# All experts but the last in fp16 halves, and a new split of the low halves between GpSimd and VectorE

## The chip, the cores and the metric

The kernel runs on one core of a Trainium2 chip. A core has TensorE (PE, matrix products into PSUM), VectorE (DVE), ScalarE (ACT), GpSimd (POOL, which reads and writes SBUF only) and SyncE (SP, which issues most of the DMAs here). Each engine works through its own queue in order and waits on semaphores for the others. The metric is the device time of one execution in microseconds (us); the median of 3 runs of the kernel before is 131.86 us (131.57 to 131.89).

## The reference

2048 tokens of 128 numbers (32 sequences of 64) pass through one attention layer and one mixture of experts:

```python
x = x + xattn(ctx, layernorm(x), Wq)          # q = xn Wq^T, k = v = ctx Wq^T, scores / sqrt(128), causal softmax in each sequence of 64
xf = layernorm(x)
logits = xf @ gate_W                          # 8 experts
gates = softmax(logits); top-2, renormalised  # cw[token, expert]
out = xf
for e in range(8):
    h = relu(xf @ W1[e] + b1[e])              # 128 -> 256
    out = out + cw[:, e:e+1] * (h @ W2[e] + b2[e])   # 256 -> 128
x = x + out
```

The kernel puts two sequences of 64 into a tile of 128 tokens, and a mask keeps them apart. It computes every expert for every token and weighs the result, so that the work does not depend on the routing.

## The kernel before, in words

The 2048 tokens are 16 tiles of 128, in four groups of four tiles (`GROUPS = 4`, 512 tokens each). Group 0's attention comes first, in a start part (roughly the first 20 us). Then a loop runs over the groups g and over the eight experts e; between the experts of group g it carries out, in small steps, the attention, the second layer norm and the router of the next groups. Where each step stands is given by slots, two for each expert: `X_T = 11`, `PROBS_T = 18` and so on are slot numbers counted from two groups earlier, 16 slots to a group. Every engine has its own table `steps` with these slots, and runs them in the same order of slots. That order is fixed by the program: no scheduler changes it.

An expert consists of:

- the hidden product on PE (`hidden_product`): for each of two halves c of the 256 hidden units, three fp16 products of 512 columns into `psH[c]`: high x high, low weights x high, high weights x low. These halves are a way to compute in nearly fp32 with fp16 operands: a number is a high part (rounded to fp16) and a low part (the rest);
- the relu on ACT (`hidden_relu`), with the bias b1 in the activation. An expert "in fp16 halves" (`is_split`) is evacuated twice for each c: `h_hi` in fp16, and `h` in fp32. A full one is evacuated once, as `h` in fp32;
- the low part of h, for split experts only: `h_lo = h - h_hi`. Half c = 0 is a subtraction on POOL (`hidden_lo0`, L690), half c = 1 one on DVE (`hidden_lo`, L848). "Low half" below means such a subtraction, 128 x 512;
- the output product on PE (`output_product`): for a split expert 24 fp16 products (h_hi with w2_hi, h_hi with w2_lo, and at the end h_lo with w2_hi, for which PE waits for both low halves); for a full one 8 fp32 products, which the trace shows as 16;
- the weighted sum on DVE (`add_expert`, L864), four instructions, one for each tile: `acc = psY * weight + acc`.

PE issues the hidden product of expert n + 1 ahead of the output product of expert n, and ACT and DVE run ahead in the same way. `FULL = (0, 3)` makes experts 0 and 3 of each group full, `FULL_LAST = (0, 7)` experts 0 and 7 of the last group.

Around the loop these matter here. On ACT: `gate_exps` (L553) waits for DVE's `below` (L805) and stands in the queue between the relu of expert 7 and that of expert 0 of the next group (in the start part between relu 0 and relu 1); `softmax` (L542) comes behind the relu of expert 1. On DVE: `gate_top`, `gate_choice` and `gate_weights` (L800 to L839) are the router, a chain of small instructions each of which waits for the one before; they stand ahead of the low half of expert 1. On POOL: the power -1/2 for the second layer norm (`attention_rstd`, L673) stands in slot 5, the sum x1 + xf (`base_sum`, L682) in slot 10, the power for the first norm (`first_rstd`, L677) in slot 12, each between low halves. DVE writes the variance that L673 waits for in L771, after the sum of expert 2.

Of the kernel before, what the change touches and what calls it, by code (L numbers as in the profile page):

```python
# [7 lines left out]
ALU = mybir.AluOpType  # L8
# [25 lines left out]
def xattn_moe(nc, x, ctx, wq, gate_w, w1, b1, w2, b2, out):  # L34
    P = 128
    BATCH, SEQ, D = x.shape
    E, _, HID = w1.shape
# [5 lines left out]
    C = HID // P  # L43
# [3 lines left out]
    SX, SW, SH = 16.0, 64.0, 16.0  # L47
    FULL = (0, 3)
    FULL_LAST = (0, 7)
    HB = 2 * C  # L50
# [12 lines left out]
    def is_split(g, e):  # L63
        return e not in (FULL_LAST if isinstance(g, int) and g == GROUPS - 1 else FULL)

    def splits(g, e):

        return g * (E - len(FULL)) + sum(is_split(g, i) for i in range(e + 1))

    stack = ExitStack()  # L70
    with stack:  # L71
# [85 lines left out]
        h = sb("h", [P, HB, GT])  # L157
# [129 lines left out]
        def _(pe):  # L287
# [102 lines left out]
            def output_product(g, e):  # L390

                n = g * E + e
# [26 lines left out]
                if split:  # L419
                    pe.wait_ge(hlo_ready, splits(g, e))  # L420
                    pe.wait_ge(hlo0_ready, splits(g, e))
                    for t in range(TG):
                        add_product(t, h_lo, w2_hi, False, last_expert or t == TG - 1)
# [223 lines left out]
        def _(pool):  # L647
# [36 lines left out]

            def hidden_lo0(g, e):

                if is_split(g, e):
                    i = C * (e % 2)
                    pool.wait_ge(h_ready, (g * E + e) * C + 1)
                    nc.gpsimd.tensor_tensor(h_lo[:, i, :], h[:, i, :], h_hi[:, i, :],  # L690
                                            ALU.subtract).then_inc(hlo0_ready, 1)

            steps = [(FIRST_RSTD, 2, first_rstd), (RSTD, 1, lambda a: attention_rstd(a, ALL)), (BASE, 1, base_sum)]

            def group(g):
                for e in range(E):
                    if e < E - 1:
                        hidden_lo0(g, e + 1)
                    elif g + 1 < GROUPS:
                        hidden_lo0(g + 1, 0)  # L700
                    run(steps, g * SLOTS + 2 * e)
                    run(steps, g * SLOTS + 2 * e + 1)
# [15 lines left out]
            base_sum(0)  # L718
            hidden_lo0(0, 0)
            for g in range(GROUPS):  # L720
# [4 lines left out]
        def _(dve):  # L725
# [118 lines left out]
            def hidden_lo(g, e):  # L844
                if is_split(g, e):
                    i = C * (e % 2) + 1
                    dve.wait_ge(h_ready, (g * E + e + 1) * C)
                    nc.vector.tensor_tensor(h_lo[:, i, :], h[:, i, :], h_hi[:, i, :],  # L848
                                            ALU.subtract).then_inc(hlo_ready, 1)
# [183 lines left out]
```

## Time and profile before

| | |
|---|---|
| median of 3 runs | 131.86 us |
| profiled execution, its own time | 130.83 us |
| its span, first to last instruction | 129.0 us |
| TensorE's granted clock | full speed in all 40 slices of the page |
| POOL, busy share of the span | 41% (53.5 us, 57 instructions) |
| ACT, busy share of the span | 73% (93.5 us, 191 instructions) |
| DMA queues together, after the weights are in | near zero, but for the stores of a group |

The profile comes from one execution. Busy times count what an engine executes, not its semaphore waits; matrix products are pipelined, so that a record of one starts before the record of the one ahead has ended, and the distance between two starts is the better measure of what one costs. The same holds for ACT's and DVE's records, which overlap by about 0.1 us. The groups of instructions give, for each line of the kernel and each tile, the count, the busy time, the mean of one and the idle time just ahead. The timeline gives the start, the length, and in brackets the idle time before with the instruction that ended it.

### The profile page before, as it was taken

What the parts mean: (1) busy time and instruction counts of PE and PEld (TensorE: products, weight loads), DVE (VectorE), ACT (ScalarE), POOL (GpSimd) and SP (SyncE); (2) the same over time, 40 slices, a digit from 0 to 9 for tenths busy, and PEclk for the clock granted to TensorE, in tenths of its full rate; (3) what the DMA queues carried; (4) which work ended last, traced back from release to release, by engine and by line L of the source; (5) the groups of instructions that cost most, each with busy time, mean ns of one, the idle gap of its engine ahead of it and who ended that gap; (6) DMA issues with size and microseconds to landing.
All of it is one profiled execution on the core that took longest, in us unless ns stands there. A gap on an engine that the chain in (4) does not pass through costs nothing. (4 is left out here: it accounts for less than half of the span.)

```text
span 129.0 us, 3295 instructions
## 1 busy us (share of the span) xinstructions
PE 120.3 (93%) x1175; PEld 90.7 (70%) x1175; DVE 107.6 (83%) x419; ACT 93.5 (73%) x191; POOL 53.5 (41%) x57
## 2 busy tenths in 40 slices
PE   6987788999979999999999999999999979999991
PEld 2585566777847768778768778778776757776690
DVE  0629998989999999989898999958998798866683
ACT  3337485999776955996779927993799467989830
POOL 7199155330094951330095640330468303345400
PEclk9999999999999999999999999999999999999999
DMA  3999900000000000200000000200000002000002
GB/s 92 321 283 321 289 26 8 0 0 0 5 0 0 0 5 3 81 0 5 0 0 5 0 3 13 68 5 0 3 0 8 0 0 86 3 0 0 5 0 81
DMA packets 9904, 5.54 MB, mean 43 GB/s; under 512 B 504, under 2 KB 9888, under 8 KB 9888
## 3 DMA queue, kind: packets, MB, share of 16 engines
q1 hardware_dynamic: 9744, 5.27, 15.2%
q8 instruction: 9, 0.15, 0.5%
q10 hardware_dynamic: 144, 0.07, 0.2%
q14 instruction: 7, 0.06, 0.1%
HBM read 4.28 MB, written 1.05 MB: 41 GB/s over the span
## 5 line engine op out<-in xcount | busy, mean ns | idle before, releaser
L690 POOL TENSOR_TENSOR h_lo<-h,h_hi 128x512 f16<-128x512 f32 x24 | 28.7, 1196 | 40.2 <-ACT h L571 39.9
L571 ACT ACTIVATE h<-psH,b1T 128x512 f32<-128x512 f32 x64 | 43.3, 689 | 1.1 <-PE psH L508 0.9
L570 ACT ACTIVATE h_hi<-psH,b1T 128x512 f16<-128x512 f32 x48 | 33.0, 688 | 11.5 <-PE psH L387 11.4
L864 DVE SCALAR_TENSOR_TENSOR acc<-psY,weight_y,acc 128x128 f32<-128x128 f32 x125 | 35.1, 342 | 1.4 <-PE psY L408 1.2
L383 PE MATMUL psH<-x_hi,w_hi 128*128 128x512 f16 x62 | 23.5, 379 | 1.0 <-ACT h L571 1.0
L387 PE MATMUL psH<-x_lo,w_hi 128*128 128x512 f16 x62 | 23.5, 379 | 0.0
L384 PE MATMUL psH<-x_hi,w_lo 128*128 128x512 f16 x62 | 23.5, 379 | 0.0
L848 DVE TENSOR_TENSOR h_lo<-h,h_hi 128x512 f16<-128x512 f32 x24 | 16.5, 689 | 7.8 <-ACT h L571 7.3
L408 PE MATMUL psY<-w_hi,h_hi 128*128 128x128 f16 x192 | 22.7, 219 | 0.0
L408 PE MATMUL psY<-w_lo,h_hi 128*128 128x128 f16 x192 | 22.7, 219 | 0.0
L408 PEld LDWEIGHTS psY<-w_hi,h_hi 128*128 128x128 f16 x192 | 15.3, 98 | 2.2
L408 PE MATMUL psY<-w_hi,h_lo 128*128 128x128 f16 x192 | 14.6, 219 | 0.8 <-POOL h_lo L690 0.8
L408 PEld LDWEIGHTS psY<-w_sb,h 128*128 128x128 f32 x116 | 14.1, 192 | 1.0
L408 PEld LDWEIGHTS psY<-w_lo,h_hi 128*128 128x128 f16 x192 | 14.7, 98 | 0.0
L408 PE MATMUL psY<-w_sb,h 128*128 128x128 f32 x116 | 14.3, 275 | 0.0
L673 POOL TENSOR_TENSOR rstd<-var,half 128x4 f32<-128x4 f32 (+1 forms) x5 | 4.7, 953 | 21.8 <-DVE var L771 21.8
L408 PEld LDWEIGHTS psY<-w_hi,h_lo 128*128 128x128 f16 x192 | 11.6, 98 | 1.0 <-issue 0.9
L387 PEld LDWEIGHTS psH<-x_lo,w_hi 128*128 128x128 f16 x62 | 6.1, 98 | 7.3
L383 PEld LDWEIGHTS psH<-x_hi,w_hi 128*128 128x128 f16 x62 | 6.1, 98 | 6.9 <-ACT h L571 3.1
L384 PEld LDWEIGHTS psH<-x_hi,w_lo 128*128 128x128 f16 x62 | 6.1, 98 | 2.8
L677 POOL TENSOR_TENSOR rstd<-mv,half 128x4 f32<-128x4 f32 x4 | 5.0, 1250 | 5.8 <-DVE mv L734 5.8
L682 POOL TENSOR_TENSOR acc<-x,xf 128x512 f32<-128x512 f32 x4 | 7.1, 1784 | 0.0
(191 smaller groups left out, 191.4 us busy)
## 6 DMA issues: line engine op xcount, KB each, us to landing
w_sb<-in_L_ffn_W_dram SPq DMA_DIRECT2D x8, 256.0 KB, 4.9
out_dram<-acc SPq DMA_DIRECT2D x3, 256.0 KB, 2.3
x_sb<-in_x_dram SPq DMA_DIRECT2D x2, 256.0 KB, 4.0
ctx_sb<-in_ctx_dram SPq DMA_DIRECT2D x2, 256.0 KB, 4.4
x_sb<-in_x_dram SPq DMA_DIRECT2D x1, 512.0 KB, 7.6
ctx_sb<-in_ctx_dram SPq DMA_DIRECT2D x1, 512.0 KB, 8.5
out_dram<-acc SPq DMA_DIRECT2D x2, 128.0 KB, 1.8
wq_sb<-in_L_xattn_Wq_dram ACTq DMA_DIRECT2D x1, 64.0 KB, 2.8
```

The lines of the kernel that those rows point to most:

```text
L383: nc.tensor.matmul(psH[c][:, :], w1_hi[:, e, w], x_hi[:, g, :], start=True, stop=False)
L384: nc.tensor.matmul(psH[c][:, :], w1_lo[:, e, w], x_hi[:, g, :], start=False, stop=False)
L387: nc.tensor.matmul(psH[c][:, :], w1_hi[:, e, w], x_lo[:, g, :], start=False, stop=True).then_inc(z_ps, 1)
L408: last = nc.tensor.matmul(o, hidden[:, C * i + c, t * P:(t + 1) * P], weights[:, e, c, :], start=start and c == 0, stop=stop and c == C - 1)
L570: nc.scalar.activation(h_hi[:, C * (e % 2) + c, :], psH[c][:, :], ACT.Relu, bias=bias, scale=scale)
L571: nc.scalar.activation(h[:, C * (e % 2) + c, :], psH[c][:, :], ACT.Relu, bias=bias, scale=scale).then_inc(h_ready, 1)
L673: nc.gpsimd.tensor_tensor(rstd2[:, v], var2[:, v], half[:, v], ALU.pow).then_inc(rstd2_ready, len(ts))
L677: nc.gpsimd.tensor_tensor(rstd[:, bass.ts(a, TG)], mv[:, bass.ts(a, TG), 1], half[:, 0:TG], ALU.pow).then_inc(rstd_ready, TG)
L682: nc.gpsimd.tensor_tensor(acc[:, bass.ts(a, TG), :], x1[:, :, :], xf[:, :, :], ALU.add).then_inc(base_ready, 1)
L690: nc.gpsimd.tensor_tensor(h_lo[:, i, :], h[:, i, :], h_hi[:, i, :], ALU.subtract).then_inc(hlo0_ready, 1)
L848: nc.vector.tensor_tensor(h_lo[:, i, :], h[:, i, :], h_hi[:, i, :], ALU.subtract).then_inc(hlo_ready, 1)
L864: last = nc.vector.scalar_tensor_tensor(out=o, in0=y, scalar=weight_y[:, g % 2, t, e:e + 1], in1=o, op0=ALU.mult, op1=ALU.add)
```

## The change

`FULL` becomes empty and `FULL_LAST` becomes `(7,)`: the experts 0 and 3 of groups 0 to 2 and expert 0 of the last group are now computed in halves; only expert 7 of the last group stays full. The first low half (c = 0) of every split expert stays on POOL. The second (c = 1) is now done by the engine that the table `LO_DVE` names, a 1 for DVE: experts 1, 4 and 5 of each group on DVE, experts 0, 2, 3, 6 and 7 on POOL. `lo_count` counts how many low halves each of the two engines has finished, for PE's waits.

```diff
--- before.py
+++ after.py
@@ -45,8 +45,9 @@
     SCALE = float(D) ** -0.5
     MASKED = 1e30
     SX, SW, SH = 16.0, 64.0, 16.0
-    FULL = (0, 3)
-    FULL_LAST = (0, 7)
+    FULL = ()
+    FULL_LAST = (7,)
+    LO_DVE = (0, 1, 0, 0, 1, 1, 0, 0)
     HB = 2 * C
     Y_FREE = 2
     SK, SV = 4.0, 64.0
@@ -63,9 +64,13 @@
     def is_split(g, e):
         return e not in (FULL_LAST if isinstance(g, int) and g == GROUPS - 1 else FULL)
 
-    def splits(g, e):
-
-        return g * (E - len(FULL)) + sum(is_split(g, i) for i in range(e + 1))
+    def lo_on_dve(n, c):
+
+        return c == 1 and LO_DVE[n % E] > 0
+
+    def lo_count(on_dve, n):
+
+        return sum(lo_on_dve(i, c) == on_dve for i in range(n + 1) if is_split(i // E, i % E) for c in range(C))
 
     stack = ExitStack()
     with stack:
@@ -417,8 +422,8 @@
                     else:
                         add_product(t, h, w2_sb, True, True)
                 if split:
-                    pe.wait_ge(hlo_ready, splits(g, e))
-                    pe.wait_ge(hlo0_ready, splits(g, e))
+                    pe.wait_ge(hlo_ready, lo_count(True, n))
+                    pe.wait_ge(hlo0_ready, lo_count(False, n))
                     for t in range(TG):
                         add_product(t, h_lo, w2_hi, False, last_expert or t == TG - 1)
 
@@ -682,22 +687,24 @@
                 nc.gpsimd.tensor_tensor(acc[:, bass.ts(a, TG), :], x1[:, :, :], xf[:, :, :],
                                         ALU.add).then_inc(base_ready, 1)
 
-            def hidden_lo0(g, e):
-
-                if is_split(g, e):
-                    i = C * (e % 2)
-                    pool.wait_ge(h_ready, (g * E + e) * C + 1)
-                    nc.gpsimd.tensor_tensor(h_lo[:, i, :], h[:, i, :], h_hi[:, i, :],
-                                            ALU.subtract).then_inc(hlo0_ready, 1)
+            def hidden_lo_pool(g, e):
+
+                n = g * E + e
+                for c in range(C):
+                    if is_split(g, e) and not lo_on_dve(n, c):
+                        i = C * (e % 2) + c
+                        pool.wait_ge(h_ready, n * C + c + 1)
+                        nc.gpsimd.tensor_tensor(h_lo[:, i, :], h[:, i, :], h_hi[:, i, :],
+                                                ALU.subtract).then_inc(hlo0_ready, 1)
 
             steps = [(FIRST_RSTD, 2, first_rstd), (RSTD, 1, lambda a: attention_rstd(a, ALL)), (BASE, 1, base_sum)]
 
             def group(g):
                 for e in range(E):
                     if e < E - 1:
-                        hidden_lo0(g, e + 1)
+                        hidden_lo_pool(g, e + 1)
                     elif g + 1 < GROUPS:
-                        hidden_lo0(g + 1, 0)
+                        hidden_lo_pool(g + 1, 0)
                     run(steps, g * SLOTS + 2 * e)
                     run(steps, g * SLOTS + 2 * e + 1)
 
@@ -716,7 +723,7 @@
                 attention_rstd(0, ts)
             first_rstd(1)
             base_sum(0)
-            hidden_lo0(0, 0)
+            hidden_lo_pool(0, 0)
             for g in range(GROUPS):
                 group(g)
 
@@ -842,7 +849,7 @@
                 dve.wait_ge(cat_ready, a + 1)
 
             def hidden_lo(g, e):
-                if is_split(g, e):
+                if is_split(g, e) and lo_on_dve(g * E + e, 1):
                     i = C * (e % 2) + 1
                     dve.wait_ge(h_ready, (g * E + e + 1) * C)
                     nc.vector.tensor_tensor(h_lo[:, i, :], h[:, i, :], h_hi[:, i, :],
```

How this stands on the engines. The first place is POOL's queue, from the second norm's power of group 0 to the first norm's power of group 2 (L673 is L678 after, L677 is L682, L682 is L687, L690 is L697). Before:

```order
L673 TENSOR_TENSOR rstd2<-var2,half 128x2 x2
L677 TENSOR_TENSOR rstd<-mv,half 128x4
L682 TENSOR_TENSOR acc<-x1,xf 128x512
L690 TENSOR_TENSOR h_lo<-h,h_hi 128x512 x2
L673 TENSOR_TENSOR rstd2<-var2,half 128x4
L690 TENSOR_TENSOR h_lo<-h,h_hi 128x512 x3
L682 TENSOR_TENSOR acc<-x1,xf 128x512
L690 TENSOR_TENSOR h_lo<-h,h_hi 128x512
L677 TENSOR_TENSOR rstd<-mv,half 128x4
```

After:

```order
L678 TENSOR_TENSOR rstd2<-var2,half 128x2 x2
L682 TENSOR_TENSOR rstd<-mv,half 128x4
L687 TENSOR_TENSOR acc<-x1,xf 128x512
L697 TENSOR_TENSOR h_lo<-h,h_hi 128x512 x7
L678 TENSOR_TENSOR rstd2<-var2,half 128x4
L697 TENSOR_TENSOR h_lo<-h,h_hi 128x512 x4
L687 TENSOR_TENSOR acc<-x1,xf 128x512
L697 TENSOR_TENSOR h_lo<-h,h_hi 128x512 x2
L682 TENSOR_TENSOR rstd<-mv,half 128x4
```

Between base_sum of group 0 and the power of group 1's second norm there were two low halves (of experts 1 and 2; expert 0 had none) and are now seven: both of 0, the first of 1, both of 2, both of 3. Behind the power four stand in place of three: the first of 4, the first of 5 and both of 6.

The second place is ACT's queue at the end of the start part: relu of expert 0, the router's exponential, relu of expert 1, and the softmax of group 1 (L570 is L575 after, L571 is L576, L553 is L558, L542 is L547). Before:

```order
L571 ACTIVATE h<-psH0,b1T 128x512
L571 ACTIVATE h<-psH1,b1T 128x512
L553 ACTIVATE gate_exp<-below 128x32
L570 ACTIVATE h_hi<-psH0,b1T 128x512
L571 ACTIVATE h<-psH0,b1T 128x512
L570 ACTIVATE h_hi<-psH1,b1T 128x512
L571 ACTIVATE h<-psH1,b1T 128x512
L542 ACTIVATE probs,row_sum<-neg_s,neg_max 128x128 x4
```

After:

```order
L575 ACTIVATE h_hi<-psH0,b1T 128x512
L576 ACTIVATE h<-psH0,b1T 128x512
L575 ACTIVATE h_hi<-psH1,b1T 128x512
L576 ACTIVATE h<-psH1,b1T 128x512
L558 ACTIVATE gate_exp<-below 128x32
L575 ACTIVATE h_hi<-psH0,b1T 128x512
L576 ACTIVATE h<-psH0,b1T 128x512
L575 ACTIVATE h_hi<-psH1,b1T 128x512
L576 ACTIVATE h<-psH1,b1T 128x512
L547 ACTIVATE probs,row_sum<-neg_s,neg_max 128x128 x4
```

Two evacuations have come in ahead of the router's exponential; what follows has kept its order.

The third place is DVE's queue behind the router of group 0: the low half of expert 1, the sum of expert 0, the low half of expert 2, a part of the weights, the sum of expert 1 (L848 is L855 after, L864 is L871, L951 is L958). Before:

```order
L839 SCALAR_TENSOR_TENSOR weight_cat<-weight,weight_cat 128x4x8
L848 TENSOR_TENSOR h_lo<-h,h_hi 128x512
L864 SCALAR_TENSOR_TENSOR acc<-psY0,weight_y,acc 128x128 x4
L848 TENSOR_TENSOR h_lo<-h,h_hi 128x512
L951 SCALAR_TENSOR_TENSOR w1_lo<-w1_sb,w1_hi 128x512
L864 SCALAR_TENSOR_TENSOR acc<-psY1,weight_y,acc 128x128 x4
```

After:

```order
L846 SCALAR_TENSOR_TENSOR weight_cat<-weight,weight_cat 128x4x8
L855 TENSOR_TENSOR h_lo<-h,h_hi 128x512
L871 SCALAR_TENSOR_TENSOR acc<-psY0,weight_y,acc 128x128 x4
L958 SCALAR_TENSOR_TENSOR w1_lo<-w1_sb,w1_hi 128x512
L871 SCALAR_TENSOR_TENSOR acc<-psY1,weight_y,acc 128x128 x4
```

The low half of expert 2 has left DVE; that of expert 1 stands where it stood, behind the router's last instruction.

## Rows read from the trace of the kernel before

**Rows 1.** The page's busy times: engine, busy us, share of the span, instructions.
```profile
PE 120.3 (93%) x1175; PEld 90.7 (70%) x1175; DVE 107.6 (83%) x419; ACT 93.5 (73%) x191; POOL 53.5 (41%) x57
```

**Rows 2.** Groups: line, engine, tiles, shapes, count, busy us, mean ns, idle before.
```profile
L570 ACT ACTIVATE h_hi<-psH,b1T 128x512 f16<-128x512 f32 x48 | 33.0, 688 | 11.5 <-PE psH L387 11.4
L690 POOL TENSOR_TENSOR h_lo<-h,h_hi 128x512 f16<-128x512 f32 x24 | 28.7, 1196 | 40.2 <-ACT h L571 39.9
```

**Rows 3.** Who waited for whom: total us, times, longest us.
```profile
ACT gate_exp L553 <- DVE below L805: 7.1, 4, 2.5
...
PE psH L383 <- ACT h L571: 1.0, 2, 0.7
...
PE psY L408 <- POOL h_lo L690: 0.8, 1, 0.8
```

**Rows 4.** PE's timeline, outputs 18 and 19: start, us, tiles; next product's start ends each.
```profile
87.83 0.28 PE L408 MATMUL psY<-w_hi,h_hi 128*128 128x128 f16 x2
...
89.17 0.38 PE L383 MATMUL psH<-x_hi,w_hi 128*128 128x512 f16 x1
...
90.46 1.95 PE L408 MATMUL psY<-w_sb,h 128*128 128x128 f32 x16
92.25 0.38 PE L383 MATMUL psH<-x_hi,w_hi 128*128 128x512 f16 x1
```

**Rows 5.** Timelines of PE and ACT, hidden product 17 to output 17.
```profile
78.85 0.38 PE L383 MATMUL psH<-x_hi,w_hi 128*128 128x512 f16 x1
...
79.69 0.69 ACT L570 ACTIVATE h_hi<-psH,b1T 128x512 f16<-128x512 f32 x1 [0.68 <-PE psH L387]
...
83.14 0.40 ACT L542 ACTIVATE probs<-neg_s,neg_max 128x128 f32<-128x128 f32 x1
...
83.85 0.28 PE L408 MATMUL psY<-w_hi,h_hi 128*128 128x128 f16 x2
```

**Rows 6.** Timelines of DVE, POOL and PE, sum of expert 18 to output 20's low part.
```profile
89.37 1.13 DVE L864 SCALAR_TENSOR_TENSOR acc<-psY,weight_y,acc 128x128 f32<-128x128 f32 x4 [0.37 <-PE psY L408]
...
91.80 0.17 DVE L771 TENSOR_SCALAR var<-mv 128x4 f32<-128x4 f32 x1
...
92.11 1.01 POOL L673 TENSOR_TENSOR rstd<-var,half 128x4 f32<-128x4 f32 x1 [6.09 <-DVE var L771]
93.08 2.54 POOL L690 TENSOR_TENSOR h_lo<-h,h_hi 128x512 f16<-128x512 f32 x2
...
94.49 0.61 PE L408 MATMUL psY<-w_hi,h_lo 128*128 128x128 f16 x8
```

**Rows 7.** Timelines of ACT, DVE, POOL and PE at the start of group 0.
```profile
20.64 1.26 ACT L571 ACTIVATE h<-psH,b1T 128x512 f32<-128x512 f32 x2 [0.92 <-PE psH L508]
...
22.67 0.67 ACT L570 ACTIVATE h_hi<-psH,b1T 128x512 f16<-128x512 f32 x1
...
26.10 0.40 ACT L542 ACTIVATE probs<-neg_s,neg_max 128x128 f32<-128x128 f32 x1
...
22.31 0.19 DVE L805 TENSOR_TENSOR below<-logits,top 128x32 f32<-128x32 f32 x1
...
24.21 1.03 DVE L825 TENSOR_TENSOR chosen<-chosen,gate_exp 128x32 f32<-128x32 f32 x1
...
26.84 0.69 DVE L848 TENSOR_TENSOR h_lo<-h,h_hi 128x512 f16<-128x512 f32 x1
...
35.44 0.17 DVE L771 TENSOR_SCALAR var<-mv 128x4 f32<-128x4 f32 x1
...
23.99 1.20 POOL L690 TENSOR_TENSOR h_lo<-h,h_hi 128x512 f16<-128x512 f32 x1 [2.90 <-ACT h L571]
...
27.70 0.61 PE L408 MATMUL psY<-w_hi,h_lo 128*128 128x128 f16 x8
```

**Rows 8.** Timelines of DVE and POOL, the router of group 1.
```profile
53.19 1.17 DVE L825 TENSOR_TENSOR chosen<-chosen,gate_exp 128x32 f32<-128x32 f32 x1
...
53.16 1.16 POOL L690 TENSOR_TENSOR h_lo<-h,h_hi 128x512 f16<-128x512 f32 x1 [4.22 <-ACT h L571]
```

## The prediction

> **What bounds the kernel now.** I read the busy times first. TensorE (PE) is busy 93% of the span, VectorE (DVE) 83% [rows 1]: PE sets the pace, and DVE is close enough behind to set it in places. Next the groups: one ScalarE (ACT) evacuation of 512 columns lasts 0.69 us, a low half costs GpSimd (POOL) 1.2 us [rows 2] and DVE 0.69 us [rows 7]. In timelines such records overlap by about 0.1 us; I count 0.57 us for one step of ACT and 0.6 us for a low half on DVE. The waits then show little idle time on PE that is put down to anyone: 0.8 us once for POOL's low half, 1.0 us in two waits for ACT's h [rows 3]. What the reader has to find is in the timelines: whether PE, where it seems to run without a gap, stands on another engine's chain with no slack. It does so in two places of every group and in one place of the start.
>
> I number experts through, n = 8g + e. Seven change: 0, 3, 8, 11, 16, 19 and 24. Only 31 stays fp32.
>
> **PE's work.** An fp32 output product runs from 90.46 to 92.25, 1.79 us; a split one from 87.83 to 89.17, 1.34 us [rows 4]. So the change takes 0.45 us of PE from each of seven experts, 3.15 us in all. It gives ACT two more evacuations each, 2 x 0.57 = 1.15 us, 8 us in all, POOL 26 more low halves (24 become 50: 31 first ones and 19 second ones), and DVE 12 fewer (24 become 12, 7 us). If all of PE's saving stayed, the profiled 130.83 us would become 127.7. I now ask of each place what comes late there.
>
> **Experts 8 and 16: the softmax chain.** The hidden product of expert 17 starts at 78.85. ACT starts on it at 79.69, having idled for it, issues four evacuations (2.3 us) and then four exponentials, the last at 83.14; PE's transposes of these end at 83.85, where output product 17 begins [rows 5]. From 78.85 to 83.85 is 5.00 us. PE's own work in it is hidden 17 1.29 (89.17 to 90.46 [rows 4]), output 16 1.79, hidden 18 1.29 and four fp32 transposes of 128 columns, which I estimate at 4 x 1.79/16 = 0.45: 4.82. The chain is already 0.18 us longer. A split output 16 makes PE's work 4.37 and changes nothing in the chain: the 0.45 us is lost. ACT's two more evacuations for 16 lie in front of 79.69. They fit only if gate_exp, which stands in ACT's queue before relu 16, comes earlier; it waits for DVE's `below` [rows 3]. DVE loses two low halves (experts 14 and 15) just before, 1.2 us, of which I count on 0.6 to 0.7. So I take 0 for this place; bounds: a loss of 0.9 where `below` doesn't come earlier, a gain of 0.1.
>
> **Experts 3, 11 and 19: the rstd chain.** DVE starts add_expert 18 at 89.37, having idled for PE, and writes the variance at 91.80; POOL takes the power from 92.11, and only then, in its queue, the low halves from 93.08; PE's low part of output 20 starts at 94.49 [rows 6]. Output 18 ended at 89.17, so the chain takes 5.32 us, and PE's work in it is 1.29 + 1.79 + 1.29 + 0.89 (the first 16 of the 24 products of 1.34 us) = 5.26. Again PE has no slack, and 0.45 us less work gives 0.45 us more wait. POOL's two new low halves of 19 are done by about 90.4 (relu 19 follows relu 18 on ACT and ends by 89.2, plus 1.2), before the power: free. In group 0 POOL's wait of 0.8 us [rows 3] stands at this place already. I take 0, bounds -0.45 to +0.3 each.
>
> **Expert 24.** PE waits 0.7 us for relu 24's first half [rows 3], since gate_exp is late. DVE without low half 23 is 0.6 us earlier; relu 24's first half now takes two evacuations, 0.57 us later, its second 1.15 us. The three cancel with the 0.45 us: 0, bounds -0.5 to +0.6.
>
> **The start: expert 0.** Here I find the cost. PE needs DVE's low half of expert 1 at 27.70, and DVE had it from 26.84 to 27.53: 0.2 us of slack [rows 7]. Ahead of it DVE has the router's chain of small instructions from `below` at 22.31 on. One of them, L825, took 1.03 us instead of 0.18: it stood beside POOL's only low half there, 23.99 to 25.19. The same pair stands at 53.19 and 53.16, where DVE's 1.17 us ends with POOL's 1.16 [rows 8]. So a small tensor-tensor operation of DVE on two SBUF inputs doesn't run while POOL subtracts, and it waits for the end of the whole instruction. DVE instructions with an input in PSUM (add_expert) beside the same POOL instructions keep their length. The Trainium skill says this in "SBUF — State Buffer", "Who interferes with whom": the pair of ports that both share is locked for a whole instruction, also by a DVE instruction with two SBUF inputs. The trace agrees with 1.17 against 0.18 us; by that rule the router's scan and scalar-tensor-tensor steps, which no row here shows blocked, wait as well.
>
> After the change POOL has, in this chain, both low halves of 0, the first of 1 and, at its end, those of 2. Step by step: relu 0 starts at 20.64 [rows 7] and has four steps, so its first half is done at 21.9, its second at 23.05. POOL subtracts from 21.95 to 23.1 and again for 1.2 us. `below`, due at 22.31, waits until 23.15: +0.85. gate_exp follows and relu 1 starts about 23.35 in place of 22.67, the exponentials and output 1 about 0.7 us later (before, the last exponential started at 26.10 [rows 7] and output 1 at 27.70 - 0.89 = 26.81). DVE from the end of `below` to the end of low half 1 took 27.53 - 22.50 = 5.03 us, less the 0.85 in L825: 4.2 us free of POOL. From 23.2 this would end at 27.4. To it come POOL's second half of 0 (1.1 us), the first half of 1 (1.1 us) and, since that brings DVE's last steps to 28.6 while relu 2 gives POOL its half at 28.5, the first half of 2 (1.1 us); less 0.3 where DVE's w2_lo holds its turn. That is 30.4. If the third is missed it is 29.5; if POOL's second half of 2 slips in as well, 31.5. PE is ready for it at 27.5 + 0.9 = 28.4. Low half 1 is thus late by 1.8, 2.8 or 3.8 us against 27.70.
>
> Some of that comes back: DVE no longer has low half 2 and its wait (0.97 us together), the b2 product's and the attention product's small waits vanish. Following DVE (add_expert 0 from 30.4, residual after PE's attention product at 33.6, add_expert 2 at 35.35), the variance of group 1 comes at 37.85 in place of 35.61 [rows 7]: +2.2; for the other two cases +1.3 and +3.3. From there the rstd chain and everything behind it hangs on that variance, so PE's shift is the same. I take the middle one.
>
> Sum on the profiled execution: 130.83 + 2.2 (start) + 0 (two softmax chains) + 0 (three rstd chains) + 0 (expert 24) = 133.0 us. The median of the runs shown is 131.86, so 1.03 above; with the same distance 134.0 us.
>
> **The rivals.**
> *The saving comes through.* PE is the busiest engine, and 3.15 us leave it. For it: everything else has spare time on average. Against it: both chains above are as long as PE's work to within 0.2 us. Price: -3.15, and +0.4 at the start (ACT's two more evacuations): 129.1; with only one kind of place giving, 130.5.
> *The start isn't blocked.* DVE's small steps slip in between POOL's halves. For it: their gaps of 0.03 us are many, and the first of four xf instructions got through between two of POOL's once. Against it: L825 was held in full each time. Then only relu 1's 0.4 us remains, partly given back: +0.2, 132.1.
> *The forecast*, slower by POOL's halves in the router's chain of the start: 134.0, its own range 133.1 to 135.2.
> *The same in every group.* From group 0 to 3 `below` meets POOL's second low half of experts 7, 15, 23. I place these 0.1 to 0.5 us before `below`. If they slip behind it, gate_exp comes 0.6 to 0.9 us late, relu 9 and 17 and the softmax chains with them: 134.0 + 2 to 2.5 = 136.3. It decides where `below` still waits at its old place.
>
> **How the numbers follow.** No change is what lies within 0.3%, 0.4 us. Forecast 0.56; in every group 0.08; start not blocked 0.18; saving comes through 0.18. Slower: 0.56 + 0.08 + 0.05 of the third = 0.69. Same: 0.12 of the third and 0.02 of the last = 0.14. Faster: 0.17. The range from 131.0 to 135.6 leaves out most of the saving case (0.13) and most of the worst one (0.07).
>
> **What would show it.** Right: `below` of group 0 at 23.1 or later and several router steps of about 1.1 us; the low half of expert 1 after 29.5, and PE waiting for it more than 1 us before its low part of output 1; in groups 1 and 2 PE's waits before output 9, 17, 12 and 20 grown by 0.45 each, with the distance from one group's rstd to the next still 27.9 us. Wrong: this distance at 27.0, or the low half of expert 1 before 28.5; or gate_exp of groups 1 and 2 no earlier against PE's hidden product before it than now.

## The result and the profile after

The changed kernel takes 135.25 us (134.9 to 135.94), the kernel before 131.88 us on the same chip: a ratio of 1.0277 [1.0236, 1.0318]. The change makes it 3.4 us slower. The profiled execution took 134.9 us with a span of 133.1 us, against 130.83 and 129.0; TensorE has its full clock in all 40 slices in both. The two traces are 4.1 us apart, a little more than the medians, and it is these 4.1 us that are divided up below. I was right that it gets slower, and right about the mechanism in the start part; the time forecast, 134.0 us, is 1.25 us short, and a second place that I had put at nothing costs 1.1 us.

Busy times of the page after, to be read against [rows 1]:

```profile
PE 119.3 (90%) x1231; PEld 86.6 (65%) x1231; DVE 106.6 (80%) x407; ACT 101.5 (76%) x205; POOL 81.7 (61%) x83
```

PE is busy for only 1.0 us less, and DVE for 1.0 us less though it has 12 low halves fewer (16.5 us of them before, 9.2 after): much of what it no longer computes it now stands blocked. ACT has the 8 us more that were counted, POOL 28 us more, with 26 more low halves. The groups of the page after, against [rows 2]:

```profile
L697 POOL TENSOR_TENSOR h_lo<-h,h_hi 128x512 f16<-128x512 f32 x50 | 59.5, 1196 | 30.9 <-ACT h L576 30.9
...
L575 ACT ACTIVATE h_hi<-psH,b1T 128x512 f16<-128x512 f32 x62 | 43.1, 696 | 9.6 <-PE psH L392 8.7
...
L855 DVE TENSOR_TENSOR h_lo<-h,h_hi 128x512 f16<-128x512 f32 x12 | 9.2, 764 | 2.3 <-ACT h L576 2.1
```

A low half on POOL costs what it did. DVE's own has risen to 764 ns in the mean, since one of the twelve lasts 1.60 us. The waits of the kernel after (who waited for whom: total us, times, longest), against [rows 3]:

```profile
ACT gate_exp L558 <- DVE below L812: 6.0, 4, 2.0
...
PE psH L388 <- ACT h L576: 2.7, 6, 0.8
PE psY L413 <- POOL h_lo L697: 2.4, 3, 1.8
...
PE psY L413 <- DVE h_lo L855: 1.7, 1, 1.7
```

PE's waits have grown: those for low halves from 0.8 to 4.1 us, those for `h` from 1.0 to 2.7. But a list of waits doesn't tell which of them reaches the end. For that I follow one and the same event of the program in both traces (start in us):

| event | before | after | later by |
|---|---|---|---|
| PE, low part of output 1 | 27.70 | 30.33 | 2.63 |
| DVE, variance of group 1 | 35.44 | 38.40 | 2.96 |
| DVE, variance of group 2 (behind softmax chain of group 1) | 63.92 | 67.44 | 3.52 |
| ACT, first exponential of the second softmax chain | 81.99 | 86.02 | 4.03 |
| PE, low part of output 20 (behind the rstd chain) | 94.49 | 98.57 | 4.08 |
| PE, last low part (expert 30) | 123.75 | 127.88 | 4.13 |

So the loss is 2.96 us in the start, 0.56 and 0.51 us at the two softmax chains, and 0.1 us in all the rest. Each place is now looked at in turn. The start, timelines of POOL, DVE and PE of the kernel after, against [rows 7]:

```profile
22.05 2.32 POOL L697 TENSOR_TENSOR h_lo<-h,h_hi 128x512 f16<-128x512 f32 x2 [0.89 <-ACT h L576]
24.74 1.61 POOL L697 TENSOR_TENSOR h_lo<-h,h_hi 128x512 f16<-128x512 f32 x1 [0.37 <-ACT h L576]
28.57 2.72 POOL L697 TENSOR_TENSOR h_lo<-h,h_hi 128x512 f16<-128x512 f32 x2 [2.22 <-ACT h L576]
```

```profile
22.38 0.87 DVE L812 TENSOR_TENSOR below<-logits,top 128x32 f32<-128x32 f32 x1
23.18 0.18 DVE L813 TENSOR_TENSOR is_second<-logits,top 128x32 f32<-128x32 f32 x1
23.28 1.11 DVE L814 TENSOR_TENSOR one_above<-top 128x4 f32<-128x4 f32 x1
...
24.67 0.67 DVE L964 SCALAR_TENSOR_TENSOR w_lo<-w_sb,w_hi 128x512 f16<-128x512 f32 x1
25.25 1.14 DVE L824 TENSOR_TENSOR nth<-nth,one_above 128x32 f32<-128x32 f32 x1
...
28.67 1.60 DVE L855 TENSOR_TENSOR h_lo<-h,h_hi 128x512 f16<-128x512 f32 x1
...
34.51 1.55 DVE L964 SCALAR_TENSOR_TENSOR w_lo<-w_sb,w_hi 128x512 f16<-128x512 f32 x1
...
38.40 0.17 DVE L778 TENSOR_SCALAR var<-mv 128x4 f32<-128x4 f32 x1
```

```profile
30.33 0.62 PE L413 MATMUL psY<-w_hi,h_lo 128*128 128x128 f16 x8 [1.71 <-DVE h_lo L855]
```

Read the lengths, not the starts: `below` takes 0.87 us in place of 0.19 and ends with POOL's first half; L814, four numbers in each lane, takes 1.11 us and ends with POOL's second half; L824 ends with POOL's half of expert 1. It is mutual: that half of expert 1 itself takes 1.61 us in place of 1.2, having started 0.07 us after DVE's w2_lo (L964, the low part of the weights W2, two SBUF inputs) of 0.67 us. Last, DVE's low half of expert 1 meets POOL's first half of 2 (1.60 us), and at 34.51 DVE's w2_lo meets POOL's second half of expert 3 (1.55 us). Between two of POOL's halves that follow each other without a pause DVE gets something through: here `below`, which had been held, and L813 right behind it.

The softmax chain between groups 0 and 1, timelines of DVE, POOL and ACT of the kernel after (it corresponds to [rows 5], which are of one group later):

```profile
49.63 1.00 DVE L741 TENSOR_SCALAR mv<-mv 128x4 f32<-128x4 f32 x1
...
52.20 0.19 DVE L812 TENSOR_TENSOR below<-logits,top 128x32 f32<-128x32 f32 x1
```

```profile
48.33 2.28 POOL L697 TENSOR_TENSOR h_lo<-h,h_hi 128x512 f16<-128x512 f32 x2
```

```profile
52.42 0.23 ACT L558 ACTIVATE gate_exp<-below 128x32 f32<-128x32 f32 x1 [1.94 <-DVE below L812]
52.55 0.67 ACT L575 ACTIVATE h_hi<-psH,b1T 128x512 f16<-128x512 f32 x1
...
55.31 0.72 ACT L575 ACTIVATE h_hi<-psH,b1T 128x512 f16<-128x512 f32 x1
...
57.58 0.46 ACT L547 ACTIVATE probs<-neg_s,neg_max 128x128 f32<-128x128 f32 x1
```

`below` itself is free (0.19 us). But ahead of it in DVE's queue, with one sum, the logits and the maxima between, stands L741, which adds a constant to four variances. It waits 0.83 us for the end of POOL's second low half of expert 7 (50.61). So gate_exp is not early, as I had counted on: it comes 2.57 us later than before (49.85), when everything around is 2.96 us later, so 0.4 us earlier, not the 0.6 to 0.7 counted. At the second chain it isn't earlier at all: counted from the start of PE's hidden product before it, gate_exp comes at 2.80 us in group 1 (3.14 before) and at 2.74 us in group 2 (2.56 before). ACT then runs from 52.42 to the exponentials with no pause ahead of relu 9 (55.31), where it used to idle for PE [rows 5, of relu 17]: the two evacuations of expert 8 are now on the path.

The rstd chain of group 2, timelines of DVE, POOL and PE of the kernel after, against [rows 6]:

```profile
93.45 1.12 DVE L871 SCALAR_TENSOR_TENSOR acc<-psY,weight_y,acc 128x128 f32<-128x128 f32 x4 [0.38 <-PE psY L413]
...
95.87 0.17 DVE L778 TENSOR_SCALAR var<-mv 128x4 f32<-128x4 f32 x1
```

```profile
96.19 1.01 POOL L678 TENSOR_TENSOR rstd<-var,half 128x4 f32<-128x4 f32 x1 [1.71 <-DVE var L778]
```

```profile
98.57 0.61 PE L413 MATMUL psY<-w_hi,h_lo 128*128 128x128 f16 x8 [0.28 <-POOL h_lo L697]
```

From the sum to the low part of output 20 it is 5.12 us, as before (94.49 - 89.37). PE has 0.45 us less work here, and the distance is the same: it waits the longer for it.

### The profile page after: what moved, and what is told of

It is laid out like the page before. It is cut to its first block and busy times, and to the rows that moved or that the text cites. A ratio compares the mean times of both kernels' runs of the same rounds, so it can differ in the third digit from the quotient of the medians.

```text
span 133.1 us, 3442 instructions
## 1 busy us (share of the span) xinstructions
PE 119.3 (90%) x1231; PEld 86.6 (65%) x1231; DVE 106.6 (80%) x407; ACT 101.5 (76%) x205; POOL 81.7 (61%) x83
## 3 DMA queue, kind: packets, MB, share of 16 engines
HBM read 4.28 MB, written 1.05 MB: 40 GB/s over the span
## 5 line engine op out<-in xcount | busy, mean ns | idle before, releaser
L697 POOL TENSOR_TENSOR h_lo<-h,h_hi 128x512 f16<-128x512 f32 x50 | 59.5, 1196 | 30.9 <-ACT h L576 30.9
L575 ACT ACTIVATE h_hi<-psH,b1T 128x512 f16<-128x512 f32 x62 | 43.1, 696 | 9.6 <-PE psH L392 8.7
L576 ACT ACTIVATE h<-psH,b1T 128x512 f32<-128x512 f32 x64 | 44.7, 699 | 0.2 <-PE psH L392 0.2
L871 DVE SCALAR_TENSOR_TENSOR acc<-psY,weight_y,acc 128x128 f32<-128x128 f32 x125 | 35.1, 341 | 7.5 <-PE psY L413 7.2
L413 PE MATMUL psY<-w_hi,h_hi 128*128 128x128 f16 x248 | 29.3, 219 | 0.0
L413 PE MATMUL psY<-w_lo,h_hi 128*128 128x128 f16 x248 | 29.3, 219 | 0.0
L413 PE MATMUL psY<-w_hi,h_lo 128*128 128x128 f16 x248 | 18.9, 219 | 4.1 <-POOL h_lo L697 2.4
L413 PEld LDWEIGHTS psY<-w_hi,h_hi 128*128 128x128 f16 x248 | 19.9, 98 | 3.8
L413 PEld LDWEIGHTS psY<-w_lo,h_hi 128*128 128x128 f16 x248 | 19.0, 98 | 0.0
L855 DVE TENSOR_TENSOR h_lo<-h,h_hi 128x512 f16<-128x512 f32 x12 | 9.2, 764 | 2.3 <-ACT h L576 2.1
L678 POOL TENSOR_TENSOR rstd<-var,half 128x4 f32<-128x4 f32 (+1 forms) x5 | 4.7, 953 | 9.5 <-DVE var L778 9.5
L791 DVE TENSOR_SCALAR xf<-x,mv,rstd 128x128 f32<-128x128 f32 x16 | 7.2, 508 | 0.0
L682 POOL TENSOR_TENSOR rstd<-mv,half 128x4 f32<-128x4 f32 x4 | 4.4, 1096 | 4.5 <-DVE mv L741 4.5
L547 ACT ACTIVATE probs<-neg_s,neg_max 128x128 f32<-128x128 f32 x16 | 6.3, 428 | 0.8 <-DVE neg_max L748 0.8
```

The costliest lines, as they stand in the source:

```text
L413: last = nc.tensor.matmul(o, hidden[:, C * i + c, t * P:(t + 1) * P], weights[:, e, c, :], start=start and c == 0, stop=stop and c == C - 1)
L547: nc.scalar.activation(probs[:, t, :], neg_s[:, t, :], ACT.Exp, bias=neg_max[:, t:t + 1], scale=-1.0, accum_out=row_sum[:, t:t + 1]).then_ ...
L575: nc.scalar.activation(h_hi[:, C * (e % 2) + c, :], psH[c][:, :], ACT.Relu, bias=bias, scale=scale)
L576: nc.scalar.activation(h[:, C * (e % 2) + c, :], psH[c][:, :], ACT.Relu, bias=bias, scale=scale).then_inc(h_ready, 1)
L678: nc.gpsimd.tensor_tensor(rstd2[:, v], var2[:, v], half[:, v], ALU.pow).then_inc(rstd2_ready, len(ts))
L791: nc.vector.tensor_scalar(xf[:, t, :], x1[:, t, :], mv2[:, t, 0:1], rstd2[:, t:t + 1], ALU.subtract, ALU.mult).then_inc(xf_ready, 1)
```

## The experiments

All are changes of the changed kernel. In the comparisons of stretches I count from the first hidden product of expert 0 in each trace, since the input's transfers move that start by up to 1.2 us from run to run. In this measure the last low part comes at 104.29 us before and at 108.35 after. A result is given as the ratio to the kernel before on the same chip with its 95% interval, and then the median.

**Where in the start.** Theory: the 3 us are POOL's halves of expert 0 in front of DVE's router. Rival: ACT's extra evacuations, or PE's changed order, cost it. Two kernels: expert 0 of group 0 left full, and its two low halves written as zeros by POOL (which leaves out that low part) with all else in place, ACT's evacuations too.

```diff
 # e3_first_full, in is_split
+        if g == 0 and e == 0:
+            return False
```

> The changed kernel, but expert 0 of group 0 full. If the start's cost (PE's low part of output 1 2.6 us later, the variance of group 1 2.9 us later) comes from expert 0's two low halves on POOL and two more evacuations, it goes nearly whole: 132.3 to 132.8 us, with the softmax chains' 0.5 us each left. Rival, the cost comes from the second half of expert 2 on POOL or from the rest of group 0: 134 us or more.

```diff
 # e4_first_memset, in hidden_lo_pool
+                        if n == 0:
+                            nc.gpsimd.memset(h_lo[:, i, :], 0.0).then_inc(hlo0_ready, 1)
+                            continue
```

> The changed kernel, but POOL writes zeros into both low halves of expert 0 of group 0 in place of subtracting (the low part of h of this one expert is left out). ACT's evacuations, PE's products and the waits are unchanged. If a subtraction on POOL blocks DVE because both read SBUF through the same port, and a write of zeros doesn't, the router's below comes at its old place, 0.9 us earlier, and one more block of 1.1 us goes: the time falls by 1.2 to 1.8 us to about 133.7. Rival 1, ACT's two more evacuations make the start's cost: unchanged, 135.2. Rival 2, any POOL instruction blocks for its own length: in between, by the length of the memset.

Measured: e3 1.0072 [1.0045, 1.0099], 132.29 us; e4 1.0136 [1.0097, 1.0174], 133.18 us. Both are about as expected. The low part of output 4 comes at 19.23 before, 22.11 after, 18.93 in e3, 19.32 in e4. POOL and DVE of e4 in the start:

```profile
22.55 0.53 POOL L698 MEMSET h_lo<- 128x512 f16 x1 [0.87 <-ACT h L576]
23.71 0.53 POOL L698 MEMSET h_lo<- 128x512 f16 x1 [0.63 <-ACT h L576]
```

```profile
22.90 0.19 DVE L815 TENSOR_TENSOR below<-logits,top 128x32 f32<-128x32 f32 x1
```

`below` runs beside a POOL instruction in 0.19 us when that one only writes. With two instructions that read replaced by two that write (and are half as long), 2.8 of the 2.9 us are gone from the trace; a fall of 1.2 to 1.8 us was expected, and by the ratios, each uncertain by 0.5 us, it is 1.9. ACT's evacuations cost next to nothing here: at the low part of output 1 the distance is 8.24 before, 8.66 in e4, 10.80 after, and by output 4 the 0.4 us have been given back but for 0.1.

**Which expert.** Theory: in groups 1 to 3 expert 3 (and 11, 19) neither costs nor gains, expert 8 and 16 cost at the softmax chains; in group 0 both meet POOL. Here only the list of full experts changes.

```diff
 # e2_pool_only: the list of before, with the new table of low halves
-    FULL = ()
-    FULL_LAST = (7,)
+    FULL = (0, 3)
+    FULL_LAST = (0, 7)
 # e5_full0
+    FULL = (0,)
+    FULL_LAST = (0, 7)
 # e6_full3
+    FULL = (3,)
+    FULL_LAST = (7,)
```

> The other half of the change alone: experts 0 and 3 full as in the kernel before, the second low halves divided between POOL and DVE by the new table. In the router's chain of the start POOL has then only the first half of expert 1, as before; so no cost there: 131.4 to 132.0 us. DVE's order to subtract the mean's variance step (mv) of the next norm is then blocked by the second half of expert 7, which eats the 0.6 us that DVE is relieved by. Rival, POOL's extra work is what costs: 133.5 us or more.

> Expert 0 of each group full, expert 3 in halves (in groups 0 to 2), low halves by the new table. Against the kernel with both full and the same table (0.9939 of the kernel before) PE has 0.45 us less in each of three groups. If the rstd chain (output 2, residual, sum 2, statistics, variance, POOL's power, POOL's low half of expert 4) holds the group, none of it arrives: a ratio of 0.992 to 0.997. Rival, the saving arrives: 1.35 us less, a ratio near 0.984.

> Expert 3 of groups 0 to 2 full, expert 0 in halves, table as in the change. The start's cost (2.9 us) and the softmax chains' (0.5 each) hang on expert 0 and stay. PE's 0.45 us more in three places is hidden by the rstd chain: 1.024 to 1.030, as the changed kernel. Rival, expert 3's halves contribute to the cost (two more low halves on POOL ahead of the power, two more evacuations): 1.02 or below. Rival, expert 3's saving did arrive: 1.036.

Measured: e2 0.9939 [0.9914, 0.9965], 130.67 us; e5 0.9934 [0.9902, 0.9967], 130.81 us; e6 1.0228 [1.0189, 1.0267], 134.43 us. e2 is the other half of the change by itself: twelve low halves moved from DVE to POOL, no expert split that wasn't. It is 0.6% faster, a gain that I had not forecast for this half alone. The trace has it in two places: 0.3 us in group 0 (low part of output 4 at 18.94), and 0.5 us at expert 24, where PE's wait for relu 24 falls from 0.72 to 0.24 us. e5 splits 3, 11 and 19 as well, 3 x 0.45 us less work for PE, and its last low part stands at 103.45 (e2: 103.46): nothing of it arrives. e6 splits 0, 8, 16 and 24 but not 3, 11 and 19. Its ratio lies between the forecast (1.024 to 1.030) and the rival (1.02 or below), and its interval overlaps that of the full change; the traces separate the two. In them e6 gains 0.86 us, all in group 0 (low part of output 4 at 21.25 against 22.11): the block of w2_lo, 1.55 us at 34.51 in the full change, is gone. DVE of e6:

```profile
35.61 0.68 DVE L964 SCALAR_TENSOR_TENSOR w_lo<-w_sb,w_hi 128x512 f16<-128x512 f32 x1
```

**Splitting by itself.** Here the table is that of the kernel before, second low half always on DVE, with all experts but the last split.

```diff
 # e1_split_only
-    LO_DVE = (0, 1, 0, 0, 1, 1, 0, 0)
+    LO_DVE = (1, 1, 1, 1, 1, 1, 1, 1)
```

> The change's split alone: every expert but the last in halves, and all second low halves on DVE, all first ones on POOL. If the start costs because POOL's low halves block the router's chain, and the softmax chains because relu 8 and 16 are two evacuations longer behind the router's exponential (gate_exp), both stay in part: start +1.5 (POOL has the first halves of 0, 1, 2, and DVE one low half more ahead of that of expert 1), softmax chains +0.9 each since DVE is not relieved ahead of gate_exp: about 135.1 us. Rival, the costs come from POOL's taking over of second halves alone: within 0.5 us of the kernel before, 131.9 us, or, with PE's saving, below it.

Measured: 1.1093 [1.1039, 1.1147], 145.5 us. The expectation missed by 10 us, the rival by 14. What neither of them had looked at is DVE's order: its low half of expert 11 now stands ahead of the residual and the variance of the next group. DVE of e1 in group 1:

```profile
67.26 0.69 DVE L855 TENSOR_TENSOR h_lo<-h,h_hi 128x512 f16<-128x512 f32 x1 [1.38 <-ACT h L576]
...
68.08 1.13 DVE L762 SCALAR_TENSOR_TENSOR x<-psA,inv_sum,x_sb 128x128 f32<-128x128 f32 x4
69.12 1.12 DVE L871 SCALAR_TENSOR_TENSOR acc<-psY,weight_y,acc 128x128 f32<-128x128 f32 x4
...
71.53 0.17 DVE L778 TENSOR_SCALAR var<-mv 128x4 f32<-128x4 f32 x1
```

The waits of e1:

```profile
DVE h_lo L855 <- ACT h L576: 18.1, 13, 2.6
POOL rstd L678 <- DVE var L778: 17.0, 4, 5.1
```

An instruction that waits for expert 11's h, which comes late, stands ahead of the chain that the whole group hangs on: from the variance of group 1 to that of group 2 it is 31.9 us, against 28.5 before. The same order stands in groups 0 and 2, with waits of 1.82 and 1.39 us there. By the last low part e1 is 13.8 us behind the kernel before: 3.4 us of it come up to the variance of group 1, 3.4 and 2.5 us up to those of groups 2 and 3, and 4.6 us behind, where PE stands still from 121.2 to 123.2 and its granted clock is at the lower level for 3.4 us from 122.8 on (0.50; mean of the execution 0.987). The 4.6 us haven't been followed further, and no run takes the order of expert 11's low half by itself: that it is the main cost is read from the traces, not shown by an experiment. So splitting alone costs 14 us, and the new table, which leaves DVE no low half of experts 3 and 11, gives 10 to 11 of them back.

**The softmax chains.** Theory: it is POOL's second low half of expert 7, through L741. Rival: ACT's two evacuations cost the same without it. In e7 POOL writes zeros for that half in groups 0 to 2 (which leaves out that low part).

```diff
 # e7_memset7, in hidden_lo_pool
+                        if e == 7 and c == 1:
+                            nc.gpsimd.memset(h_lo[:, i, :], 0.0).then_inc(hlo0_ready, 1)
+                            continue
```

> The changed kernel, but POOL writes zeros as the second low half of expert 7 of groups 0 to 2 in place of subtracting (this low part is left out). In the changed kernel that subtraction holds DVE's instruction mv (1.0 us in place of 0.17) ahead of the sum of expert 6 and of the router. If gate_exp is late for that reason, and relu 8 and 16, two evacuations longer, push relu 9 and 17 by 0.5 us for it, gate_exp comes 0.8 us earlier and the softmax chains start again on PE's product: 1.0 us less in all, a ratio near 1.020. Rival, ACT's load alone makes the softmax chains late: unchanged, 1.0277.

Measured: 1.0198 [1.0164, 1.0233], 134.14 us. POOL and DVE of e7:

```profile
49.86 0.52 POOL L698 MEMSET h_lo<- 128x512 f16 x1
```

```profile
50.07 0.34 DVE L744 TENSOR_SCALAR mv<-mv 128x4 f32<-128x4 f32 x1
```

The instruction (L744 here, L741 in the changed kernel) falls from 1.00 to 0.34 us, the first exponential of the chain comes 0.56 us earlier than in the changed kernel (37.49 against 38.05), and the chains cost nothing any more: from variance to variance it is 28.4 and 27.9 us, as in the kernel before. The last low part comes 1.17 us earlier, and the time is as expected. ACT's evacuations alone thus cost nothing: gate_exp now comes at 2.01 and 1.94 us from PE's hidden product before it, early enough for them, as the prediction had it.

**The rstd chain.** If the groups hang on the variance, one slot earlier for it must give time back. The step `VARIANCE` is put before the sum of expert 2 in place of behind it.

```diff
 # e8_early_var, and in e9, e10, e11, e12
-    ..., VARIANCE, ... = ..., 21, ...
+    ..., VARIANCE, ... = ..., 20, ...
```

> The changed kernel with DVE's statistics and variance of the second norm one slot earlier, ahead of the sum of expert 2 in place of behind it. The sum (1.05 us) and its wait for output 2 leave the rstd chain, so that its slack becomes about 1 us. If that chain is what swallows expert 3's 0.45 us, three of them arrive, and in group 0 the wait of 0.75 us that the kernel before had too: 1.4 to 2.1 us less, a ratio of 1.011 to 1.017. Rival, the chain isn't what holds PE there: unchanged.

Measured: 1.0224 [1.0183, 1.0266], 134.54 us: less than I expected, and by the times alone not clear of the changed kernel's 1.0277 [1.0236, 1.0318]. The traces show where it stands: in groups 1 and 2 it gives 0.45 us each, as expected. In group 0 only 0.28 us arrive, and 0.17 us of them are lost again by output 9, so that 1.00 us is left at the last low part. DVE of e8 there:

```profile
38.83 1.60 DVE L958 SCALAR_TENSOR_TENSOR w_lo<-w_sb,w_hi 128x512 f16<-128x512 f32 x1
...
41.06 1.32 DVE L855 TENSOR_TENSOR h_lo<-h,h_hi 128x512 f16<-128x512 f32 x1
```

DVE's w1_lo and its low half of expert 4 now meet POOL's halves: 1.60 and 1.32 us in place of 0.69.

**Kernels that might beat both.** e9 is e2 with the earlier variance; e10 is e5 with it; e11 is e10 with expert 4's second low half on POOL; e12 is e10 with expert 3 of group 0 full.

```diff
 # e9_pool_early_var: e2's lists, VARIANCE at 20
 # e10_full0_early_var: e5's lists, VARIANCE at 20
 # e11_full0_early_var_lo4: e10 and
+    LO_DVE = (0, 1, 0, 0, 0, 1, 0, 0)
 # e12_best: e10 and, in is_split
+        if g == 0 and e == 3:
+            return False
```

> Experts 0 and 3 full, low halves by the new table, the variance of the second norm one slot earlier. With expert 3 full PE's own work in the rstd chain is 5.26 us against 5.32, so shortening the chain gives nothing in groups 1 and 2; in group 0 PE's wait of 0.75 us ahead of the low part of output 4 goes in part, 0.3 us as in the changed kernel with the early variance: a ratio of 0.990 to 0.994, against 0.9939 without it. Rival, the variance's place has a gain of its own: below 0.985.

> Only expert 0 full (and the very last), low halves by the new table, the early variance. Now expert 3's 0.45 us of PE meets a chain with slack: 0.45 in each of groups 1 and 2, 0.3 in group 0, 1.2 us less than the same kernel without the early variance (0.9934): 0.984 to 0.986, the fastest so far. Rival, the saving is taken by the next chain (sum, xf, its transposes, x_lo): 0.993.

> As the run before, with the second low half of expert 4 on POOL too. In the changed kernel with the early variance DVE's low half of expert 4 ended late in group 0, behind a weights' low part that POOL blocked. On POOL it comes about 1.2 us after the first half, which is early now: in group 0 0.3 us less, elsewhere nothing: 0.982 to 0.985. Rival, POOL's second subtraction is then the late one: xf on DVE is blocked once more and the ratio rises to 0.987 or more.

> Group 0 with experts 0 and 3 full, where the weights' low parts crowd DVE and POOL's halves of expert 3 block them; groups 1 and 2 with expert 0 alone full; low halves by the new table, early variance. In the run with expert 0 alone full and the early variance the stretch from the softmax to output 4's low part was 0.44 us shorter in groups 1 and 2 than without it, and group 0 lost 0.8. So 0.44 twice off the run with both full and the early variance (0.9893): a ratio of 0.982 to 0.984. Rival, expert 3's saving doesn't arrive: 0.989.

| kernel | ratio to before | median us | last low part |
|---|---|---|---|
| e9 | 0.9893 [0.9856, 0.9930] | 129.85 | 103.14 |
| e10 | 1.0025 [0.9997, 1.0052] | 131.77 | 103.42 |
| e11 | 0.9912 [0.9874, 0.9950] | 130.63 | 103.08 |
| e12 | 0.9971 [0.9938, 1.0004] | 131.37 | 102.32 |

e9 is the fastest kernel, 1.1% below the kernel before; its last low part comes 0.31 us ahead of e2's, as expected, though by the times alone the two aren't separated. The other three missed what I expected of them. e10 gains the 0.44 us in each of the later groups against e5, and loses 0.81 us in group 0, where the variance of group 1, now earlier, meets POOL's halves of expert 3. DVE and POOL of e10:

```profile
34.48 1.05 DVE L778 TENSOR_SCALAR var<-mv 128x4 f32<-128x4 f32 x1
...
37.09 1.59 DVE L958 SCALAR_TENSOR_TENSOR w_lo<-w_sb,w_hi 128x512 f16<-128x512 f32 x1
```

```profile
33.20 2.31 POOL L697 TENSOR_TENSOR h_lo<-h,h_hi 128x512 f16<-128x512 f32 x2 [1.55 <-ACT h L576]
```

e12 avoids this and is 0.82 us ahead of e9 at the last low part, as expected; yet it is 1.0 us slower over all (0.0078 of 131.5). That loss lies behind the last sum. SP's waits, first e12, then e9:

```profile
SPq L78 <- DMA out_dram<-acc: 3.3, 1, 3.3
```

```profile
SPq L76 <- DMA out_dram<-acc: 1.5, 1, 1.5
```

The last sum ends at 125.44 and the span at 129.5 in e12, 4.1 us; in e9 at 125.63 and 127.9, 2.3 us. SP's last wait is 3.3 or 3.4 us in e10, e11 and e12, and 1.4 or 1.5 us in ten other traces that end with the same stores (before, after, e2 to e9). The DMA queues from the issue of the last stores to the end (packets, MB, share of 16 engines) and the stores themselves (KB each, median us from issue to landing), e12 and then e9:

```profile
q1 hardware_dynamic: 544, 0.26, 15.7%
q8 instruction: 1, 0.02, 1.6%
out_dram<-acc SPq DMA_DIRECT2D x2, 128.0 KB, 2.9
```

```profile
q1 hardware_dynamic: 544, 0.26, 16.0%
out_dram<-acc SPq DMA_DIRECT2D x2, 128.0 KB, 1.8
```

In e10, e11 and e12, and in none of the ten others, a packet of the instruction queue falls into this window. It takes 1.6 us in e12, and 32 of the stores' 512 packets of 512 B start 0.6 to 1.7 us behind the last of the others (at 127.56 to 128.64, the others by 126.92). Before, e2 and e9 have nine such packets in all; the other seven have a tenth too, but it came before the stores were issued. That the packet delays the stores is argued from this coincidence, three traces against ten, and not tested by an experiment of its own. At 1.8 to 1.9 us, 1.4%, it is the size of what e12 missed of its expectation (1.7 to 2.0 us); in e10 it comes on top of group 0's loss. It doesn't explain e11: the profiled execution of e11, with the packet, took 132.61 us, its seven others 129.67 to 130.96, as if without it. What e11 missed is in the trace ahead of the stores: its last low part, 103.08, is only 0.06 us ahead of e9's, since the variance at 34.47 is held for 1.05 us in group 0 there too. By the Trainium skill ("Runtime: NRT & Kernel Launch", Instruction fetch mechanics) instructions are fetched in blocks of 16 KiB and this is mostly hidden; the size fits the 0.02 MB here; if the packet is what delays the stores, the hiding doesn't hold at the end of e12.

## Why the prediction was right, and where it was short

- **PE's saving goes nowhere: right.** Of seven times 0.45 us nothing arrives. At the rstd chain 5.12 us are 5.12 us; e5 against e2 shows it for expert 3, e4 and e7 for expert 0 and for 8 and 16, where the low parts behind come no earlier than before even without the blocks. e8 shows the other side: with the sum taken out of the rstd chain, PE's 0.45 us arrive in groups 1 and 2.
- **The start: mechanism right, and right in size up to the low half of expert 1.** Forecast: `below` done at 23.15, relu 1 from 23.35, low half 1 done at 30.4. Trace: 23.25, 23.42 and 30.27. e4 shows that it is POOL's reading, not ACT's two evacuations. The scalar-tensor-tensor steps that no row had shown blocked are blocked as well (w2_lo 1.55 us in place of 0.67, and in e4 the step L838 on four numbers a lane 0.84 in place of 0.16), as the prediction had said; the scan was held in no run.
- **The start's second part: the term was mis-sized.** I had the variance end at 37.85, +2.2; it ended at 38.57, +2.96. I followed DVE from low half 1 to the variance by its waits for PE and left out POOL's halves of expert 3, which hold w2_lo (0.68 us in e6, 1.55 here) for 0.87 us. e6 takes them away and gets 0.86 us back. The same rule that I had used 10 us earlier applied here; I didn't go through the rest of DVE's queue with it.
- **The softmax chains: the step failed.** I took 0, since DVE's two missing low halves would bring gate_exp 0.6 to 0.7 us forward, and I looked at `below` alone as the one that POOL could hit. It was L741, a little ahead of it in the queue, that was hit, for 0.83 us. The price was 0.56 and 0.51 us, inside the bound of 0.9. e7 removes the hit and with it the cost. The rival "the same in every group" thus had the right instruction on POOL and the wrong one on DVE, and half its price.
- **Expert 24: 0, right** (the distance grows by 0.05 us from output 20 to the end). e2 shows the first of the terms that were to cancel by itself: with DVE relieved and expert 24 still full, 0.5 us are gained there; the split takes them back.
- The sum on the profiled execution was 133.0 and should have been 134.9: 0.76 from the start, 1.07 from the softmax chains, 0.1 from the rest. The errors all have one sign. The time of 135.25 us lies just above the forecast's own range (133.1 to 135.2) and inside the whole one (131.0 to 135.6). What brought it past its own range is half the cost of the rival "the same in every group", which I had given a chance of 0.08; that the sum still held within the whole range was in part luck.
- **The signs.** Those of the start came in: `below` done at 23.25, low half 1 at 30.27, PE's wait 1.71 us. Two of the others did not. The distance from one group's variance to the next was to stay at 27.9 us: it is 29.04 and 28.43, against 28.48 and 27.88 before, 0.56 and 0.55 longer. And gate_exp of group 2 is later against PE's hidden product than before (2.74 against 2.56 us), which I had named as a sign of being wrong.
- **The other rivals.** "The saving comes through" fell with e5. "The start isn't blocked": its 0.4 us for relu 1 is what e4 shows at output 1, but the block is there.

## What to carry to other kernels

Before moving work to GpSimd, go through VectorE's queue beside every place where GpSimd will now be subtracting, down to instructions on four numbers, and ask which of them stand on a chain; each is worth up to a whole GpSimd instruction, not its own length. Less work for the busiest engine gains nothing where a chain through other engines is as long as its work to within the saving: measure that chain first, and shorten it rather than the work (in e8 the earlier variance lets 0.45 us through in each of two groups). And test the two halves of a change apart: here the table of low halves gains 0.6%, the splitting beside it costs 3.4%, and the splitting without it 10.9%.

## What the runs showed of the hardware that was not expected

- **A tensor-scalar step is held as well.** L741 and L778 have one tensor of four numbers a lane as input, and took 1.00 and 1.05 us beside a subtraction of POOL, against 0.17. I had thought of two SBUF inputs only. The Trainium skill ("SBUF — State Buffer", Who interferes with whom) has it: `tensor_scalar` can run in a mode that uses both ports, and then contends. By that section a POOL instruction that only writes doesn't contend with a step of two inputs, and the trace agrees (0.19 us in e4); one of the two-port kind may still wait for it, and in e7 L744 (0.34 us) ends at 50.41, 0.03 us behind the memset's end at 50.38.
- **Back-to-back halves let a short instruction through.** In the start DVE lost 0.7, 0.95 and 0.95 us to three halves of POOL, not one long stop of 3.5 us. And POOL waits too: 1.61 us in place of 1.16.
- **POOL's power doesn't hold DVE, at least not over its second half**: in group 2 of the changed kernel it runs from 96.19 for 1.01 us, and DVE's low half that starts beside it, at 96.71, took 0.69 us, its usual length. The kernel before has the same pair at 92.11 and 92.63. A POOL instruction that reads SBUF and is busy for 1.01 us thus isn't always a block of 1.01 us.
- **The last stores took 1.8 to 1.9 us longer in three of the profiled executions**, with an instruction packet beside them: two kernels can differ by 1.4% in what happens after their last sum. That the packet is the cause is not shown.
